# Key-value sums kept by head and multiplied in four row parts, with gate rows, key transposes, output-gate evictions and the second value tile moved, in an mLSTM block with a ternary feed-forward

## What is computed

```python
xn = layernorm(x)
q, k = xn @ Wq.T, xn @ Wk.T            # 8 heads x 32
v, o = xn @ Wv.T, xn @ Wog.T           # 8 heads x 64, and 512
i, f = softcap(xn @ Wig.T + big), softcap(xn @ Wfg.T + bfg)
# per head, over time: C = F*C + I * k v^T ; n = F*n + I * k ; h = (q C) / max(|q n|, exp(-m))
y = (sigmoid(o) * headnorm(h) * gamma) @ Wout.T
x1 = x + y
out = x1 + ternary(w2) applied to gelu(layernorm(x1) @ ternary(w1).T + b1) + b2
```

## Time and profile before

| | before |
|---|---|
| median of 3 runs | 1897.43 us |
| lowest, highest | 1897.35, 1898.04 us |
| profiled execution | 1898.05 us |
| its span, first to last instruction | 1896.3 us |
| TensorE (PE) busy | 1829.0 us, 96% |
| VectorE (DVE) | 1231.2 us, 65% |
| ScalarE (ACT) | 1034.1 us, 55% |
| GpSimd (POOL) | 625.7 us, 33% |
| mean granted TensorE clock | 0.98 |

### The profile page before, as it was taken

One profiled execution on the slowest core, in us unless ns is written; L12 is line 12 of the kernel. 1 busy time (PEld: TensorE's weight loads), 2 busy tenths in 40 slices (PEclk: granted clock), 3 DMA queues, 4 the chain that ended last, 5 costly groups with the idle time before them and its releaser, 6 DMA issues.

```text
span 1896.3 us, 28994 instructions
## 1 busy us (share of the span) xinstructions
PE 1829.0 (96%) x11260; PEld 966.7 (51%) x11260; DVE 1231.2 (65%) x2259; ACT 1034.1 (55%) x1711; POOL 625.7 (33%) x447
## 2 busy tenths in 40 slices
PE   5779999999999999999999999999999999999989
PEld 3364544545455464645546464554645455464544
DVE  6877575675767667575765757576575756746542
ACT  6657647274563727456372745737275473736523
POOL 1534133433414343241434324143432324333230
PEclk8769999999999999999999999999999999999989
DMA  7423224251422425042251513325141432413010
GB/s 276 161 80 96 57 71 111 51 137 25 113 51 54 134 49 139 23 115 51 51 137 45 134 32 104 62 51 137 45 124 35 103 71 51 115 42 102 12 40 22
DMA packets 233512, 156.78 MB, mean 83 GB/s; under 512 B 195088, under 2 KB 199312, under 8 KB 228256
## 3 DMA queue, kind: packets, MB, share of 16 engines
q1 hardware_dynamic: 231792, 151.79, 31.2%
q10 hardware_dynamic: 1584, 3.15, 0.5%
HBM read 90.48 MB, written 17.24 MB: 57 GB/s over the span
## 4 chain that ended last, share of the span: by engine, by line
PE 76%; DVE 11%; ACT 7%; issue 2%; DMA 0%; POOL 0%; SPq 0%; POOLq 0%; DVEq 0%; ACTq 0%
PE pf L1736 23%; PE pf L1722 21%; PE pa L1612 17%; PE pa L1594 5%; PE ph L1695 4%; ACT dec L855 2%; PE ph L1689 2%; ACT L875 1%; DVE g L1188 1%; DVE g L1186 1%; DVE mean L1115 1%; ACT gT L758 1%; DVE xres L1332 1%; PE ps L1671 1%; PE ph L1653 1%
## 5 line engine op out<-in xcount | busy, mean ns | idle before, releaser
L1736 PE MATMUL pf<-w2T,gT 128*128 128x512 f16 x2048 | 535.2, 379 | 0.0
L1722 PE MATMUL pf<-x2T,w1T 128*128 128x512 f16 x2048 | 457.4, 381 | 3.4 <-ACT g L875 2.8
L1348 DVE SCALAR_TENSOR_TENSOR gT<-g,wscale,gT 128x512 f16<-128x512 f32 x256 | 192.1, 750 | 205.6 <-ACT gT L878 204.2
L1722 PEld LDWEIGHTS pf<-x2T,w1T 128*128 128x128 f16 x2048 | 194.5, 98 | 237.7 <-ACT g L875 5.9
L1736 PEld LDWEIGHTS pf<-w2T,gT 128*128 128x128 f16 x2048 | 224.4, 111 | 173.8
L1612 PE MATMUL pa<-wT,xT 128*128 128x512 f16 x1152 | 256.3, 381 | 1.9 <-DVE qT L1164 1.2
L568 POOL TENSOR_TENSOR dec<-dec,causal 128x1024 f32<-128x1024 f32 x64 | 170.2, 2690 | 248.1 <-DMA dec<-gate_r 248.1
L875 ACT ACTIVATE g<-pf,b1c 128x512 f32<-128x512 f32 x256 | 175.7, 686 | 86.8 <-PE pf L1722 86.6
L883 ACT ACTIVATE ktok<-kT 128x512 f32<-128x512 f32 x64 | 40.3, 630 | 325.6 <-DVE kT L1286 325.6
L1695 PEld LDWEIGHTS ph<-vaug,dec 128*128 128x128 f32 x1024 | 184.4, 195 | 19.9
L878 ACT ACTIVATE gT<-g,wscale 128x512 f16<-128x512 f32 x256 | 184.8, 722 | 8.4
(11 more groups left out here) (211 smaller groups left out, 2358.4 us busy)
## 6 DMA issues: line engine op xcount, KB each, us to landing
dec<-gate_r SPq DMA_DIRECT2D x32, 1024.0 KB, 6.4
xin<-L_attn_x SPq DMA_DIRECT2D x16, 1024.0 KB, 6.1
out<-x1b SPq DMA_DIRECT2D x64, 256.0 KB, 2.2
xres<-L_attn_x SPq DMA_DIRECT2D x16, 512.0 KB, 6.1
xres<-L_attn_x SPq DMA_DIRECT2D x32, 256.0 KB, 3.6
qw<-gate_w SPq DMA_DIRECT2D x128, 48.0 KB, 5.9
gT<-L_ffn_w SPq DMA_DIRECT2D x5, 1024.0 KB, 4.9
gT<-L_ffn_w ACTq DMA_DIRECT2D x3, 1024.0 KB, 5.6
```

The costliest lines, as they stand in the source:

```text
L1348: nc.vector.scalar_tensor_tensor(gT[:, LO, f, :], g32[:, f % 2, :], wscale[:, W_GELU:W_GELU + 1], gT[:, HI, f, :], ALU.mult, ALU.subtract) ...
L1722: last = nc.tensor.matmul(bank, w1T[:, k, tok(f)], x2T[:, part, :, k, :], start=(k == 0 and part == HI), stop=(k == KD - 1 and part == LO))
L1736: last = nc.tensor.matmul(bank, gT[:, part, f, tok(t)], w2T[:, f, :], start=(f == 0 and part == HI), stop=(f == NF - 1 and part == LO), sk ...
```

## The change

1. The state is stored by head without the block diagonal (`cst` is 128 x 2 x 65 per chunk), VectorE writes it there itself, and `own_head`, `spread_state` and the semaphore `c_ok` go. `chunk_state` does eight fp32 products of 32 rows by 65 columns, each in its own quarter of TensorE's rows, instead of two of 128 rows by 260 columns. The head outputs lie in four banks, one for each row part: `ps` and `ph` are now the two halves of one tensor `psh`.
2. The gate rows `gi`, `gf` lie in `sig`. `keys` no longer waits for the gate exponential, and in sequences with a feed-forward beside them K0 is evicted before the last two gate exponentials.
3. All three key chunks are transposed together before the O tiles; the third goes to bank 1 of `ps`, and its use of `pa` goes.
4. ScalarE does decay(6) before the evictions of O2 and O3. The scores of heads 2 and 3 now follow O2 and O3 directly in `pa`.
5. V1 goes to bank 1 of `ps`.
6. In sequence 0 the weights of V go through four banks, those of gates, QK and O through three, and those of the output projection through the two banks of `pa`, with waits between them and the next sequence's transposes, which share these banks.

The diff, cut to its core:

```diff
-    U_GATE, U_V, U_K, U_Q, U_O, U_KLAST = 0, 1, 3, 5, 7, 11
-    U_S = U_KLAST + 1
+    U_GATE, U_V, U_K, U_Q, U_O, U_S = 0, 1, 2, 4, 6, 10
-    PS_USES = (1 + HG, HG)
+    PS_USES = (1 + HG, 2 + HG)
...
-        cst = sb("cst", [P, T - 1, HG, H4 * VA])
+        cst = sb("cst", [P, T - 1, HG, VA])
-        gi, gf = kT[0:NH, 0, :], kT[0:NH, 1, :]
+        gi, gf = sig[0:NH, 0, :], sig[0:NH, 1, :]
-        pa, pf, ps, ph = pb("pa"), pb("pf"), pb("ps"), pb("ph")
+        pa, pf = pb("pa"), pb("pf")
+        psh = ctx.enter_context(nc.psum_tensor("psh", [P, H4, 512], F32))
+        ps, ph = psh[:, 0:2, :], psh[:, 2:4, :]
-        wbank = [ps[:, 0, :], ps[:, 1, :], pf[:, 0, :], pf[:, 1, :]]
+        wbank = [ps[:, 0, :], pf[:, 0, :], pf[:, 1, :], ps[:, 1, :], pa[:, 0, :], pa[:, 1, :]]
         def w_bank(n):
-            return n % 2 if n in USES_OUT else n % 4
+            if n in USES_OUT:
+                return 4 + (n - USES_OUT[0]) % 2
+            return n if n in USES_V else (n - USE_GATE) % 3
... gpsimd
                 weigh_queries(b)
-                for j in range(T - 1):
-                    spread_state(b, j)
                 head_norm(b, 0)
... scalar, gates(b, fb)
                 if fb is not None:
                     tokens2_hi(fb, HALVES[0])
+                    keys(b, 0)
                 act.wait_ge(gate_dve, at(b, 4, 4))
... scalar, keys
-                act.wait_ge(gate_act, at(b, 5, 5))
... scalar, sequence
-                    keys(b, 0, 1)
+                    keys(b, 1)
...
                 decay(b, 4)
+                decay(b, 6)
                 output_gate(b, 2, 3)
-                decay(b, 6)
... vector
             def state(b, j):
-                    nc.vector.tensor_copy(states[:, 0, :, :], ph[:, :, 0:VA]).then_inc(ph_free, 1)
+                    nc.vector.tensor_copy(cst[:, 0, :, :], ph[:, :, 0:VA]).then_inc(ph_free, 1)
             def head_stats(b, j, ch):
-                if j == 1:
-                    dve.wait_ge(c_ok, at(b, T - 1, T - 1))
... vector, sequence
                 keys_first(b)
+                keys_last(b)
... tensor, weights
-                    if n >= 4:
+                    if w_taken(n) > 0:
                         pe.wait_ge(s_wfree[w_bank(n)], w_taken(n))
... tensor
+            def key_tokens_all(b):
+                for n in range(HG):
+                    pe.wait_ge(pa_free[(U_K + n) % 2], pa_done(b, U_K + n))
+                if not (isinstance(b, int) and b == 0):
+                    pe.wait_ge(ps_free[0], at(b, PS_USES[0], 0))
+                    pe.wait_ge(ph_free, at(b, PH_USES, 0))
+                pe.wait_ge(ps_free[1], at(b, PS_USES[1], 1))
+                key_tokens(0, ps[:, 0, 0:QK])
+                key_tokens(1, ps[:, 0, QK:2 * QK])
+                key_tokens(2, ps[:, 1, 0:QK]).then_inc(ps_fill, 1)
... tensor, chunk_state
                 if j > 0:
-                    pe.wait_ge(c_ok, at(b, T - 1, j))
                     for g in range(HG):
-                        nc.tensor.matmul(ph[:, g, 0:H4 * VA], qw[:, g, tok(j - 1)], cst[:, j - 1, g, :],
-                                         start=True, stop=False, skip_group_check=True)
+                        for h in range(H4):
+                            own = slice(h * DQ, (h + 1) * DQ)
+                            nc.tensor.matmul(psh[:, h, g * VA:(g + 1) * VA], qw[own, g, tok(j - 1)], cst[own, j - 1, g, :],
+                                             start=(g == 0), stop=False, skip_group_check=True)
... tensor, chunk_head
-                last = nc.tensor.matmul(ph[:, g, i * VA:(i + 1) * VA], dec[:, h, tok(j)], vaug[:, j, h, :],
-                                        start=(j == 0 and i == 0), stop=(i == H4 - 1), skip_group_check=True)
+                last = nc.tensor.matmul(psh[:, i, g * VA:(g + 1) * VA], dec[:, h, tok(j)], vaug[:, j, h, :],
+                                        start=(j == 0 and g == 0), stop=(g == HG - 1), skip_group_check=True)
... tensor, sequence
                 def between(q, *uses):
                     if first:
                         ternary2_transpose(q)
+                        if uses:
+                            for n in (x_index(b + 1, 0), x_index(b + 1, 1)):
+                                pe.wait_ge(pa_free[n % 2], n // 2 + 1)
                         weights(*uses)
                 def transpose_next(*ks):
                     if first:
+                        weights_ready(*(USES_OUT[k] for k in ks))
                         transposes(b + 1, ks)
```

More of the change, by code:

```diff
@@ L97, in block_program @@
     PA_USES = U_Y + T
-    PS_USES = (1 + HG, HG)
+    PS_USES = (1 + HG, 2 + HG)
+    F_V, F_KEYS, F_SCORES = range(3)
+    PS_FILLS = F_SCORES + HG
     U_F1, U_F2 = 0, NF
@@ L213, in block_program @@
         s_wfill = sem("s_wfill")
-        s_wfree = [sem(f"s_wfree{n}") for n in range(4)]
+        s_wfree = [sem(f"s_wfree{n}") for n in range(6)]
         s_abs = sem("s_abs")
@@ L1247, in state @@
                 for g in range(HG):
-                    last = nc.vector.scalar_tensor_tensor(states[:, j, g, :], states[:, j - 1, g, :], fcol[:, g, j - 1:j],
+                    last = nc.vector.scalar_tensor_tensor(cst[:, j, g, :], cst[:, j - 1, g, :], fcol[:, g, j - 1:j],
                                                           ph[:, g, 0:VA], ALU.mult, ALU.add)
@@ L1384, in sequence @@
                 if run_f:
-                    keys_last(b)
                     if ahead:
@@ L1605, in late_values @@
                     pe.wait_ge(ph_free, at(b, PH_USES, 0))
-                token_products(ph[:, t - 2, :], xT[:, :, t, :, :], C_V).then_inc(ph_fill, 1)
+                if t == 1:
+                    if not (isinstance(b, int) and b == 0):
+                        pe.wait_ge(ps_free[1], at(b, PS_USES[1], 0))
+                    bank, fill = ps[:, 1, :], ps_fill
+                else:
+                    bank, fill = ph[:, t - 2, :], ph_fill
+                token_products(bank, xT[:, :, t, :, :], C_V).then_inc(fill, 1)
             def token_products(bank, src, col):
@@ L1643, in outer @@
                 if j == 2:
-                    pe.wait_ge(pa_free[U_KLAST % 2], pa_done(b, U_KLAST))
+                    pe.wait_ge(ps_free[1], at(b, PS_USES[1], 2))
                 if j == 0:
                     pe.wait_ge(ps_free[0], at(b, PS_USES[0], 1))
-                    for t in (0, 1):
-                        pe.wait_ge(pa_free[(U_V + t) % 2], pa_done(b, U_V + t))
+                    pe.wait_ge(pa_free[U_V % 2], pa_done(b, U_V))
+                    pe.wait_ge(ps_free[1], at(b, PS_USES[1], 1))
                     pe.wait_ge(ph_free, at(b, PH_USES, U_V2 + 2))
@@ L1662, in scores @@
                         take_pa(b, score_use(n))
-                    elif not (isinstance(b, int) and b == 0 and n == 1):
+                    else:
                         pe.wait_ge(ps_free[n % 2], ps_done(b, n) - 1)
@@ L1829, in sequence @@
                 chunk(0, 0, 1)
+                if first:
+                    for n in (score_use(NH - 2), score_use(NH - 1)):
+                        pe.wait_ge(pa_free[n % 2], pa_done(b, n))
                 prepare(*USES_OUT[0:2])
```

67 lines of the change are left out of this document (24 added, 43 removed).

## The result

The changed kernel takes **1904.31 us** (median of 16 executions, 1898.00 to 1911.95); the kernel before takes 1898.04 us (16 executions beside them, 1896.78 to 1899.62). The ratio is 1.0035, with an interval of 1.0023 to 1.0046. I forecast 1892.8 us and a range of 1882 to 1902: the time is outside the range, and on the other side of no change. The executions of the changed kernel lie 14 us apart, those of the kernel before 2.8 us. That spread is a result too.

The account below looks back on a forecast made before the run. The prediction took TensorE, busy 1829.0 of 1896.3 us, as the bound. Gains of 8.3 + 2.8 + 8.7 = 19.8 us less sequence 0's losses of 8.0 + 7.2 = 15.2 gave 4.6 us less: 1892.8 us, range 1882 to 1902.

Parts of the forecast that it names:

- The wait before Q0: TensorE's wait for K0's eviction goes in 13 steady sequences, 0.64 us each: 8.3 us gained.
- The wait for the first GELU: With decay(6) before O2 and O3's evictions, the third upward product's 0.19 us wait goes: 2.8 us gained.
- Key transposes: Third key chunk transposed elsewhere on the same queue, VectorE weighing it earlier in idle time: zero gain or loss.
- State products: Each later chunk's state in sixteen row-part instructions takes 0.68 us instead of 0.88, 45 times: 8.7 us gained.
- B: State products: the parts stream at the low end, 0.40 us a chunk, total 1879.9; chance 0.10.
- C: State products: the parts wait for one another, at least 0.88 us a chunk, total 1901.5 or up to 1949; chance 0.15.
- D: State products: parts run together but steps last 0.13 us, 0.74 us a chunk, total 1895.5; chance 0.12.
- Steady period: From one sequence's first gate product to the next: near 110.1 us in all sequences.
- Sequence 0, first part: QK's fourth weight tile waits for its bank, V2 and V3 behind it: 8.0 us lost, bounds 3 and 10.
- Sequence 0, second part: Output projection's weights share `pa` with the next sequence's transposes, which wait: 7.2 us lost, bounds 4 and 9.
- Rival A: Idle places in ScalarE's and VectorE's queues in sequence 0 leave only 7 of 15.2 us lost, total 1884.6; chance 0.18.

Follow-up runs that it names:

- experiment 8: The kernel before with only the keys' part: gate rows in the output-gate buffer, keys without their wait, K0 evicted before the last gate exponentials; 1888.24 us, ratio 0.9949.
- Experiment 1: The changed kernel, but VectorE's low parts of the next sequence's tokens wait until GpSimd has done all four masks; 1898.29 us, ratio 0.9999.
- experiment 3: The changed kernel, but in sequence 0 QK's fourth weight tile is transposed after V2 and V3 instead of before; 1897.50 us, ratio 0.9992.
- experiment 4: The changed kernel, but in sequence 0 the output weights' transposes come earlier, kept away from the next sequence's transposes; 1890.71 us, ratio 0.9963.

## Why the prediction failed

Three terms of the sum failed. Two belong together: the evictions put behind decay(6) as if the last mask were always in time, and the keys' weighing moved forward at no cost; their late masks cost 4.7 us in the profile. The third is the clock, left out of the second part of sequence 0, where it is worth up to 5.9 us and the loss is 3.4 us over the forecast. The other terms came out, within 1 us each.

- **The wait before Q0**: right. 8.3 us forecast; it is gone in all sequences, and experiment 8 shows 8.15 by the periods alone.
- **The wait for the first GELU**: right in size (0.19 us a period was there to gain; with the other gains made, undoing the order costs 0.48), wrong in its conditions. This is the first step that failed. I wrote that the scores have "1.7 us to spare" and that "decay(6) needs the last mask, which ends at 742.09, about when ScalarE gets there". The spare time is right: in sequence 8 decay(6) begins 3.2 us later than usual (35.17 against 31.98 us into the period) and the scores 1.3 us later, so 1.9 were absorbed. But "about when" was read from one sequence. In the trace of before the masks end between 30.99 and 33.28 us into the period (32.16 in the earlier trace rows), and there it cost nothing, since no bank hung on it. I put a wait that varies by 2 us ahead of two evictions and allowed it no variation.
- **Key transposes**: "VectorE weighs it earlier, in idle time", all at zero. VectorE had the time, but the instruction behind it, the 2.28 us of low parts, came forward with it: before it began 34.98 us into the period (744.91 in sequence 6), now at 31.69 in sequence 7 and 30.64 in sequence 8, from behind the masks onto the last of them. Its price, 2.1 us of GpSimd's time, is what turns a late load from 33.0 into 35.1. Experiment 1 takes away this alone and gets 6.0 us back. The prediction put this term at zero, and it was in none of the rivals.
- **State products**: 0.70 us measured, 0.68 forecast; 45 x 0.177 = 8.0 us for 8.7. The step of 0.11 us stands, as read above; that the fp32 weight load sets it is argued, since no run parts the load from the product. Rivals B (0.40), C (0.88 and more) and D (0.74) fall; D is nearest. The rule of the Trainium skill, "TensorE: Matmul & The Clock Gate", section "Measured speedup vs the span model", gives 3.07 for four row parts, and worked out from it, as an estimate, 0.75 us: the measurement lies between, nearer to the row.
- **Steady period**: 110.1 forecast, 110.03 measured. The waits and the state stage explain 0.64 + 0.19 + 3 x 0.177 = 1.36 of the 1.45 us; 0.09 a sequence have no name.
- **Sequence 0, first part**: 8.0 forecast, 8.9 measured. Right, by its own chain: TensorE waits 10.78 us at QK's fourth tile, V2 at 45.88, the scores behind O3's eviction (1.8 forecast; sequence 0 is 1.5 shorter in experiment 1).
- **Sequence 0, second part**: 7.2 forecast, 10.6 measured, above my bound of 9. The waits came (4.93 and 3.70 us, less the 4.0 that stood there before); what the sum left out is the clock. I had put 1 us for it in the first part, and none here, where the rows add up to 5.9. None of the loss was needed: with the banks as they are, the reorderings of experiments 3 and 4 take out 20.1 us, and sequence 0 had lost 19.4 (149.68 - 130.25). Rival A, that the start absorbs its waits, falls.

Forecast and result differ by 8.2 us in the profiled execution (1901.67 - 1893.45): 4.4 from sequence 0 and 4.7 from late masks, less 1.0 from the steady part and the end, with 0.1 of rounding. The median has 2.6 us more, which is the size of one more late mask; that executions differ by the number of these, and by how many of them halve the clock, is argued from the sizes and from experiment 1, since only one execution was profiled. The mean granted clock speaks for the second: it is 0.974 in the shortest of the sixteen executions (1898.00 us) and 0.969 or 0.970 in the three longest (1908.66 to 1911.95). Without the late masks the kernel would have come out level with before (experiment 1: 0.9999), so the sign of the forecast failed on sequence 0 already; the masks made level into slower, and they put the median outside 1882 to 1902, where 1898.29 would have been inside.

Open: why the gate rows land late in some sequences. They are issued 16.38 us into the period in sequences 7 and 8 alike. It happens in the kernel before as well (masks from 22.37 and 22.56 us in sequences 4 and 13). The profiles give a lead. The first load of gate rows in sequence 7 and in sequence 8 (size, us from issue to landing), and what the DMA queue q8 carried while the loads of sequence 8 were on their way (959.3 to 965.3 us; packets, MB, share of the engines):

```profile
dec<-gate_r SPq DMA_DIRECT2D x1, 1024.0 KB, 4.6
...
dec<-gate_r SPq DMA_DIRECT2D x1, 1024.0 KB, 5.8
...
q8 instruction: 1, 0.02, 1.0%
```

One packet of 16 KB, of the kind that the profile calls instruction, falls among the load's; sequence 7 has none. Over the ten profiles, sequences 1 to 15 each, the masks begin more than 21.9 us into the period in 22 of 150 sequences. In all 22 such a packet starts while the first load is on its way, and the load takes 5.5 to 6.9 us; in the 121 sequences without one it never takes more than 5.03. In seven sequences the packet does no harm (4.2 to 4.9 us). It also explains why the late sequences are nearly the same from kernel to kernel: in the eight built on the change, sequence 8 has it each time and is late each time, and sequence 12 is late in six. This is a coincidence without an exception, not an experiment: no run moved the packet or the load, and changing the order of SyncE's transfers was not tried.

## What to carry to other kernels

Before an eviction is put behind something that depends on a load, read the spread of that load's landing over all repetitions, not one, and what else the DMA queues carry when it is late; then ask who hangs on the eviction's bank. When an instruction becomes ready earlier, cost what follows it on the same engine too: it also moves, perhaps onto another engine's critical instruction. And where a change shares banks in a stage that runs once, put the products ahead of the wait in the queue, and count the clock with every new idle stretch of TensorE.

## What the runs showed of the chip that I had not expected

- **VectorE and GpSimd exclude one another here, and the later one pays.** The mask that began at 973.62 us, 0.02 behind VectorE's 2.28 us instruction, took 4.48 us instead of 2.35: 2.13 more, nearly the whole overlap. In an ordinary sequence the victim is GpSimd's next product, 3.79 us (at 864.77) instead of 1.81. In experiment 1 it is the other way round: GpSimd's product began first and took 1.80, and VectorE's low parts took 3.89 instead of 2.28:

```profile
976.97 1.80 POOL L573 TENSOR_TENSOR qw<-qw,qT 128x768 f32<-128x768 f32 x1
...
977.03 3.89 DVE L1139 SCALAR_TENSOR_TENSOR gT<-xin,gT 128x2048 f16<-128x2048 f32 x1 [2.31 <-POOL dec L563]
```

  The Trainium skill's page "SBUF — State Buffer", section "Who interferes with whom", says that a VectorE instruction with two inputs in SBUF contends with a GpSimd instruction that reads SBUF, and that the order of issue decides which of the two is blocked. The three cases agree: the later one loses 2.13 of 2.26 us of overlap, 1.98 of 2.12 and 1.61 of 1.74.
- **Two waits of 1 us can cost nearly four.** Two waits of about 1 us, 1.8 us from the one's end to the other's, left the clock at 1.00 in the changed kernel's profile and halved it for 3 us in that of experiment 3, with 1.69 us lost. It fell in six of eleven such places. Which it will be, none of these rows foretells: with first waits of 1.34 and 1.28 us it stayed up, with 1.05 and 1.10 it fell.
- **A step of four fp32 row parts takes as long as one fp32 instruction on the full array.** The steps are 0.11 us, as in the earlier trace rows for one instruction of the same 65 columns, and the sixteen take 0.61 us to the next product; the order of the parts changes this by 0.01 us.
